# Folding the first-layer biases into the weights, one wide GELU a tile, and longer lags in a sorted two-expert kernel

## What is computed

```python
n  = layernorm(x)                               # over 128 features
a  = eps * n + adj @ n                          # per graph, 256 x 256
h  = a @ gW1 + gb1                              # 128 -> 512
h  = silu(h * rsqrt(mean(h^2) + 1e-6) * rms_w)
x  = x + h @ gW2 + gb2                          # 512 -> 128

xn = layernorm(layernorm(x)) * gamma + beta
logits = xn @ Wr + br                           # 8 experts
top 2 of the logits, softmax over the two -> w
for each expert e:                              # 128 -> 256 -> 128
    y += w[e] * (gelu(xn @ W1[e] + b1[e]) @ W2[e] + b2[e])
x  = x + y
```

## Time and profile before

| | us |
|---|---|
| median of 3 runs | 474.85 (474.79 to 475.16) |
| the profiled execution's own time | 477.58 |
| its span (first to last instruction) | 475.8 |
| PE, DVE, ACT, POOL busy | 420.9, 333.8, 294.6, 242.4 |
| mean granted TensorE clock | 0.948 |

### The profile page before, as it was taken

How to read it: one execution, slowest core, us unless ns; L and a number is a source line. 1 busy time by engine, 2 the same in 40 slices (tenths; PEclk the granted TensorE clock), 3 DMA queues, 4 the chain that set the end, 5 groups by cost and what they waited for, 6 DMA issues and landing times.

```text
span 475.8 us, 12331 instructions
## 1 busy us (share of the span) xinstructions
PE 420.9 (88%) x2944; PEld 362.1 (76%) x2944; DVE 333.8 (70%) x1398; ACT 294.6 (62%) x814; POOL 242.4 (51%) x315
## 2 busy tenths in 40 slices
PE   0969999999999999999957775999999999999980
PEld 0537777777777777877747674999989989999980
DVE  5646688887777888767847365678878878677760
ACT  1235677766666776667647342788878877555540
POOL 1112246666566766665755436356555555444550
PEclk9979999999999999999997858799999999999995
DMA  6791393323322330111145304355555543333000
GB/s 200 208 300 53 125 315 106 101 95 109 100 81 91 102 106 32 36 46 48 46 137 146 91 26 121 100 148 141 143 141 145 146 122 104 104 104 92 34 39 6
DMA packets 40892, 52.21 MB, mean 110 GB/s; under 512 B 5940, under 2 KB 35764, under 8 KB 40312
## 3 DMA queue, kind: packets, MB, share of 16 engines
q1 hardware_dynamic: 31040, 28.87, 22.3%
q0 software_dynamic: 6096, 18.52, 10.7%
q10 hardware_dynamic: 3688, 4.05, 2.8%
HBM read 36.71 MB, written 22.31 MB: 124 GB/s over the span
## 4 chain that ended last, share of the span: by engine, by line
PE 77%; DVE 8%; issue 5%; another core or an unknown queue 2%; DVEq 1%; POOL 1%; ACTq 1%; DMA 1%; ACT 1%; POOLq 0%
PE banks L678 16%; PE banks L691 16%; PE banks L556 11%; PE banks L579 10%; PE banks L543 6%; PE banks L566 5%; PE banks L597 3%; PE banks L557 3%; PE banks L589 3%; PE banks L660 2%; DVE xg L941 2%; DMA eps_col<-eps 1%; ACTq L771 1%; POOL out L501 1%
## 5 line engine op out<-in xcount | busy, mean ns | idle before, releaser
L824 ACT ACTIVATE hidden_e<-banks,b_cols 128x128 f32<-128x128 f32 x368 | 106.6, 368 | 66.8 <-PE banks L678 43.7
L501 POOL DMA_INDIRECT out<-result,rows_in x92 | 89.1, 969 | 91.0 <-DVE result L1358 84.4
L691 PE MATMUL banks<-w_sb,hidden_e 128*128 (+1 forms) x736 | 102.0, 284 | 0.2 <-issue 0.2
L691 PEld LDWEIGHTS banks<-w_sb,hidden_e 128*128 128x128 f32 x736 | 93.9, 200 | 0.8 <-issue 0.6
L464 POOL DMA_INDIRECT rows_dram<-rows_out,row_of x64 | 65.0, 1015 | 23.9 <-issue 17.3
L579 PE MATMUL banks<-gw_sb,hidden_t 128*128 128x128 f32 x512 | 69.5, 279 | 0.0
L556 PE MATMUL banks<-gw_sb,agg 128*128 128x512 f32 x128 | 68.5, 618 | 0.7 <-ACT agg L765 0.7
L579 PEld LDWEIGHTS banks<-gw_sb,hidden_t 128*128 128x128 f32 x512 | 64.3, 194 | 0.9
L742 ACT ACTIVATE hidden<-banks 128x512 f32<-128x512 f32 x64 | 38.2, 597 | 42.6 <-PE banks L557 39.4
L1344 DVE SCALAR_TENSOR_TENSOR acc<-banks,rows_in,acc 128x128 f32<-128x128 f32 x92 | 32.1, 348 | 43.5 <-PE banks L691 25.9
L907 DVE TENSOR_TENSOR hidden<-banks,rms_bc 128x512 f32<-128x512 f32 x64 | 43.8, 686 | 19.8 <-ACT hidden L742 19.8
(11 more groups left out here) (129 smaller groups left out, 737.2 us busy)
## 6 DMA issues: line engine op xcount, KB each, us to landing
rows_in<-rows_dram SPq DMA_DIRECT2D x92, 132.5 KB
adj<-adj_t SPq DMA_DIRECT2D x16, 512.0 KB, 3.7
x_tok<-x SPq DMA_DIRECT2D x16, 256.0 KB, 2.9
rows_dram<-idle_in POOLq DMA_DIRECT2D x1, 3710.0 KB, 14.2
rows_dram<-idle_in SPq DMA_DIRECT2D x28, 132.5 KB
out<-result,rows_in POOLq DMA_INDIRECT x92
w_sb<-w ACTq DMA_DIRECT2D x1, 1024.0 KB, 5.6
rows_dram<-rows_out,row_of POOLq DMA_INDIRECT x64
```

Source lines behind the costliest of these rows:

```text
L501: nc.gpsimd.indirect_dma_start(out=out, out_offset=bass.IndirectOffsetOnAxis(ap=rows_in[:, i % RING][:, IDX_AT:IDX_AT + 1].bitcast(U32), a ...
L691: last = pe.matmul(y_ps(i)[:, w], hidden_e[:, i % 4, w * HCE + c], w2_sb[:, bass.ds(at + c * D, D)], start=(c == 0), stop=(c == HCE - 1))
L824: last = nc.scalar.activation(hidden_e[:, i % 4, w * HCE + c], h_ps(2 * i + w)[:, c], ACT.Gelu, bias=b1_cols[:, bass.ds(at + c, 1)])
```

## The change

Every normalised row of 128 sums to zero. A constant added to all its elements therefore drops out against weights whose columns sum to zero, and columns that sum to something else turn that constant into a bias. The change uses this to put gb1 into gW1, and gamma, beta and b1 into W1; gamma goes into Wr, and beta @ Wr into br. The constant 1 is added where ACT copies `agg` and the turned tile (`Identity` with a bias column of ones).

```diff
-                pe.matmul(hid_ps[:, n % 3], agg[...], gw1_sb[:], start=True, stop=False)
-                pe.matmul(hid_ps[:, n % 3], bias_sel[:], bias1_parts[:], start=False, stop=True
+                pe.matmul(hid_ps[:, n % 3], agg[...], gw1_sb[:], start=True, stop=True
                           ).then_inc(hid_done, 1)
```

The sums are made on PE. The first runs before everything else in PE's queue and waits for the loads of gW1, gb1 and rms_w; the four for the experts run in steps 7 to 10, behind `aggregate`:

```diff
+            def sum_weights():
+                pe.wait_ge(wide_in, WIDE)
+                pe.wait_ge(parts_made, 1)
+                pe.matmul(hid_ps[:, 2], minus_part[:], gw1_sb[:], start=True, stop=False)
+                pe.matmul(hid_ps[:, 2], row_part[:], gb1_row[:], start=False, stop=True).then_inc(sums_done, 1)
+            def sum_beta():          # step 4, one product of 8 columns
+            def sum_expert_weights(q):
+                if q == 0:
+                    pe.wait_ge(weights_in, WEIGHTS)
+                pe.wait_ge(xg_ready, q + FOLD_AT - 4)
+                pe.matmul(feat_ps, fold_by[:], w1_sb[:, q * GT:(q + 1) * GT], start=True, stop=True
+                          ).then_inc(fold_summed, 1)
```

SP issues the expert loads, ahead of x of group 6; b1 is now broadcast to all partitions (1 MB). ACT takes over both `expert_input` (as a plain copy between its last `square` and its last `keep_turned`) and the move of the turned tile:

```diff
+                    act.wait_ge(xt_turned, i + 1)
+                    nc.scalar.activation(xg_t[:, i % 4], xt_ps(i), ACT.Identity, bias=ones[:, 0:1]
+                                         ).then_inc(xg_t_ready, 1)
-                    for w in range(2):
-                        at = expert(words, i, HCE, w == 0)
-                        act.wait_ge(h_done, 2 * i + w + 1)
-                        for c in range(HCE):
-                            last = nc.scalar.activation(hidden_e[:, i % 4, w * HCE + c], h_ps(2 * i + w)[:, c],
-                                                        ACT.Gelu, bias=b1_cols[:, bass.ds(at + c, 1)])
-                        last.then_inc(gelu_done, 1)
+                    act.wait_ge(h_done, i + 1)
+                    nc.scalar.activation(hidden_e[:, i % 4], h_ps(i), ACT.Gelu).then_inc(gelu_done, 1)
```

```diff
+WIDE_LAG, NARROW_LAG, SUM_LAG = 2, 4, 4
+AHEAD = 8
-                if (i := tile_at(step, 1)) is not None:
+                if (i := tile_at(step, WIDE_LAG)) is not None:
-                if (i := tile_at(step, 2)) is not None:
+                if (i := tile_at(step, NARROW_LAG)) is not None:
```

In `tail`, the work of group 15 from `route` on moves one step later (the table's words from step 13 to 14); on POOL `shares(NG - 1)` stands behind three results instead of six, and the scatters of group 14 ahead of the first result:

```diff
-            send_result(0)
-            send_result(1)
-            send_rows(NG - 2, (0, 1))
-            send_result(2)
-            send_rows(NG - 2, (2, 3))
-            send_result(3)
...
+            send_rows(NG - 2, (0, 1, 2, 3))
+            for i in range(3):
+                send_result(i)
             shares(NG - 1)
```

More of the change, by code:

```diff
@@ L102, in expert, with build @@
     return taken.with_bounds(min_val=0, max_val=(E - 1) * width)
-def build(nc, x, adj_t, eps, gw1, gb1, rms_w, gw2, gb2_wide, gamma, beta, wr, br, w1, b1_by_chunk, w2, b2,
+def build(nc, x, adj_t, eps, gw1, gb1, rms_w, gw2, gb2_wide, gamma, beta, wr, br, w1, b1, w2, b2,
           fixed_in, upto_in, idle_in, out):
@@ L698, in _ @@
             pe.wait_ge(table_ready, 2)
-            for step in range(TILES + 2):
+            for step in range(TILES + NARROW_LAG):
                 if step == 4:
@@ L797, in _ @@
                     square(g2, 3)
+                if g4 is not None:
+                    expert_input(g4)
                 if g3 is not None:
@@ L829, in _ @@
+                if (i := tile_at(step, WIDE_LAG)) is not None:
+                    if i >= 4:
+                        act.wait_ge(y_done, i - 3)
+                    act.wait_ge(h_done, i + 1)
+                    nc.scalar.activation(hidden_e[:, i % 4], h_ps(i), ACT.Gelu).then_inc(gelu_done, 1)
             act.wait_ge(table_ready, 2)
-            for step in range(TILES + 1):
+            for step in range(TILES + WIDE_LAG):
                 if step == EARLY:
@@ L836, in _ @@
                     normalise2(NG - 1, (2, 3))
+                if step == 4:
+                    expert_input(NG - 1)
         @block.vector
@@ L1169, in _ @@
                     weigh(g2, 1)
+                if s == 3:
+                    prep_router(1)
+                if s == 4:
+                    prep_router(2)
+                if s - FOLD_AT in range(FOLDS):
+                    fold_experts(s - FOLD_AT, 0)
                 if turned:
@@ L1337, in tile_step @@
+                    if i >= AHEAD:
+                        dve.wait_ge(result_ready, i - AHEAD + 1)
+                    nc.vector.scalar_tensor_tensor(acc[:, i % AHEAD], b2_bc[:, bass.ds(expert(words, i, D, True), D)],
                                                    rows[:, bass.ds(expert(words, i, 1, True) + W_AT, 1)],
                                                    rows[:, X2_AT:X2_AT + D], ALU.mult, ALU.add).then_inc(based, 1)
-                    tail(step, 1)
-                if (j := tile_at(step, 2)) is not None:
+                tail(step, 0)
@@ L1341, in tile_step @@
+                if (j := tile_at(step, SUM_LAG)) is not None:
+                    if j < NT and j % PER_WORD == 0:
+                        done_words[j // PER_WORD % 2] = dve.value_load(word[0:1, j // PER_WORD:j // PER_WORD + 1],
+                                                                       min_val=0, max_val=2 ** 24 - 1)
                     done = rows_in[:, j % RING]
                     dve.wait_ge(base_done, j + 1)
-                    dve.wait_ge(y_done, 2 * j + 2)
-                    nc.vector.scalar_tensor_tensor(acc[:, j % 4], y_ps(j)[:, 0],
-                                                   done[:, bass.ds(expert(words, j, 1, True) + W_AT, 1)],
-                                                   acc[:, j % 4], ALU.mult, ALU.add).then_inc(low_added, 1)
@@ L1347, in tile_step @@
[L1347 removed]
+                    dve.wait_ge(y_done, j + 1)
+                    nc.vector.scalar_tensor_tensor(acc[:, j % AHEAD], y_ps(j)[:, 0],
+                                                   done[:, bass.ds(expert(done_words, j, 1, True) + W_AT, 1)],
+                                                   acc[:, j % AHEAD], ALU.mult, ALU.add).then_inc(low_added, 1)
+                tail(step, 1)
                 if i is not None:
                     dve.wait_ge(based, i + 1)
[L1350 removed]
+                    nc.vector.scalar_tensor_tensor(acc[:, i % AHEAD], b2_bc[:, bass.ds(expert(words, i, D, False), D)],
@@ L1358, in tile_step @@
                     nc.vector.scalar_tensor_tensor(result[:, j % SENDS], y_ps(j)[:, 1],
-                                                   done[:, bass.ds(expert(words, j, 1, False) + W_AT, 1)],
-                                                   acc[:, j % 4], ALU.mult, ALU.add).then_inc(result_ready, 1)
+                                                   done[:, bass.ds(expert(done_words, j, 1, False) + W_AT, 1)],
+                                                   acc[:, j % AHEAD], ALU.mult, ALU.add).then_inc(result_ready, 1)
+                tail(step, 3)
                 tail(step, 4)
+            done_words = {}
             dve.wait_ge(table_ready, 2)
-            for step in range(TILES + 2):
+            for step in range(TILES + SUM_LAG):
                 if step == EARLY:
```

281 lines of the change are left out of this document (163 added, 118 removed).

## The result

The changed kernel takes **462.77 us** (median of 4 runs, 462.02 to 463.52) against 474.84 beside it: ratio **0.974** (95% interval 0.973 to 0.976), 12.1 us less. The forecast was 441, range 429 to 455. It was measured once more later: 464.51 against 474.75, ratio 0.979 (0.974 to 0.984). The profiled execution took 462.02 us, its span is 460.2 (before 475.8).

What follows compares the result with a forecast made beforehand. PE was taken as the bound in the group stage and near its floor in late tiles, with no engine full in the first tiles. Terms summed to -34.1 us from 477.6, less 2.7 for the median: 441 us, range 429 to 455.

Steps and rivals of the forecast that it cites:

- Bias product gone and xg moved: Group stage: dropping PE's bias products saves all 14.3 us; moving xg from VectorE to ACT saves 1.0.
- Which engine moves: Moves out of PSUM: ACT faster than VectorE for f32, 590 against 810 ns at 512 wide, against the skill page's rule.
- Folding: Steps 7 to 10: four PE products and a small beta product cost 3.5 us, eight VectorE operations 1.0.
- Start: Before the groups: earlier first Silu -4.2 us, no half-speed PE clock -2.3, two new front products with the clock -0.5.
- First tiles: First 17 tile steps: half of a possible 18 us gain taken, -9.0, bounds +4 and -18.
- the unnamed waits: First tiles: waits of 4.32 and 3.77 us for code or data, which may return and speak against the gain.
- Late tiles: Later 74 tile steps: pace falls to PE's floor, less 1.7 us for word reads; -7.3 us, between -9 and +8.
- The floor: Late tiles: PE's eight products and a transpose back to back, 1.89 us per tile.
- The end: After the last tile: last product, two additions and a scatter unchanged, 0 us.
- Profile against median: Whole kernel: the median of the runs taken as 2.7 us below the profiled time, 443.5 to 440.8.
- First tiles keep their pace: Rival, first 17 tile steps: DVE, POOL and scatters set their order, not ACT, so no gain there; 450 us, chance 0.20.
- the pace of the transposes from the 18th on: Sign in the late tiles: transposes 1.9 us apart from the 18th on.

Runs made afterwards that it cites:

- the trace with late bursts: Kernel with one register, rms apart, short lags, with results of the last 28 tiles scattered six at a time; on a chip with waits 479.78 us, ratio 1.011.

## Why the prediction was wrong

By its own steps, with what each measured.

*Bias product gone and xg moved (-14.3 and -1.0).* The mechanism was right, the size too large: 13.0 a step against 13.8, 0.8 each where 0.96 was forecast, and in three of the kernel before's steps, which took 13.4, only 0.4. From the ninth tile's widening to the first transpose the two terms gave 9.3 us; their share of the forecast was 13.5. This 4.2 us is the largest part of what is missing before the tiles. The sum took the 3.0% of the chain that the bias products had as time that would all be won.

*Which engine moves.* Right. The 512-wide move takes 595 ns on ScalarE and the 128-wide with a bias column 364, against 810 and 402 on VectorE. The Trainium skill, page "ScalarE: Activation LUTs", section "Rules for kernel authors", puts additions and multiplications on VectorE; the figure that it gives as the reason is for bf16 operations with a single source, and for these f32 moves out of PSUM the trace has ScalarE faster after the change as before it.

*Folding (+3.5 and +1.0).* 2.9 us, 1.6 less than forecast. Which part is PE's product and which VectorE's chain isn't separated: the run without folding left out both.

*Start (-4.2, -2.3, -0.5).* The half-speed stretch and the wait for Silu went. The two front products put the first aggregation 3.2 us later, where the sum had -0.5 for them and the clock together. They started late, behind a broadcast of rms that they don't need. But PE did get its full pace sooner, and by the ninth tile's widening 7.0 us were won of 8.8 forecast (the three terms, and 1.8 for eight bias products): 1.8 short. With the 4.2 above and the 1.6 that folding cost less, these are the 4.4 us missing before the tiles.

*First tiles (-9.0): this step failed.* It read idle shares and estimated a pace, and the unnamed waits stood in it as one doubt among several. They are the stage: three waits of 4 to 6 us with half-clock spells behind them, which no part of the change touches. Without them, on the other sort of chip, the 17 steps take some 43 us. 3 of the 6 us that the traces show there are only moved, since the longer lags leave three half tiles for the end.

*Late tiles (-7.3): this step failed,* and it is the largest miss, 7.8 us. The sentence that failed is "DVE loses the 0.40 move and waits on nothing new but y". The new lag brought a second load of the word into a second register, and with it register work for two of four additions, which no busy column holds: 5.5 to 7.4 us, all in tiles 20 to 63. In tiles 64 to 91, which have no such work, the pace fell from 1.99 to 1.90 as forecast. The floor itself was right, 1.896 a tile, and is reached wherever VectorE's queue has room and no waits stand in the way. The wide GELU's price was right too, 598 ns for 590. What kept the kernel before above the floor stays open. Four GELUs without the bias column (0.79 us a tile) keep it with long lags, and the wide one keeps it with short lags, both on a chip without waits. Four GELUs at their old price of 1.16 together with short lags are only in the kernel before, of which there is no trace from such a chip.

*The end (0).* Wrong by 3.3 us. A pipeline that is one step and two steps deeper has three half tiles more to empty, 2.7 us, and I had not counted them.

*Profile against median.* 3.5 us. I carried the 2.7 by which the profiled execution of before exceeded its median over to the new kernel, where the profiled execution was 0.7 below.

*The rivals.* "First tiles keep their pace" (450) came nearest, 13 us off, and with the reason I gave for it, the unnamed waits. None had VectorE's queue in the tile stage. Of the signs that the prediction named only the pace of the transposes from the 18th on failed, 2.02 us instead of 1.9.

What stays open: why a burst of scatters brings such a wait, and why on some chips only. The Trainium skill, page "Runtime: NRT & Kernel Launch", section "Instruction fetch mechanics", says that each engine fetches its code through a DMA queue of its own. A fetch stuck behind scatters would stop an engine from issuing. Against it the rows above have PE issuing for a microsecond into the wait, and in the trace with late bursts the two queues that carry instructions (q8, q14) start no packet between 418.9 and 433.4 nor between 433.4 and 452.7 us, and VectorE's waits from 426.2 to 430.2 and from 442.6 to 447.2 lie in between. So these two did not end with a fetch; for the others that isn't settled. How the changed kernel itself, unedited, does on a chip without waits wasn't measured either.

## What to carry to other kernels

Where addresses come out of registers, read an engine's queue entries in the chain of waits beside its busy time, and look at the compiled program for register instructions that an edit adds: VectorE was 68% busy in the late tiles (27.32 of 40 us from 340 to 380) and yet the bound, and in the kernel before its busy time fell when it got more work in its queue. A longer lag costs its depth once at the end, and on the chip without waits it was worth nothing. A share of the chain is the most that leaving a product out can give, not what it will give. An unnamed wait of several microseconds in the profile is a term of its own, to be forecast as "stays" until an experiment moves it, and a ratio measured on one chip should be looked at on a second.

## What the runs showed of the hardware that was not expected

- Six scatters of a 128-row tile 1.26 us apart, in tiles that otherwise run at PE's pace: on one sort of chip no effect (PE 10.00 of 10 us busy), on the other some 4 us in which VectorE and ScalarE see no product done, and PE 6.42 of 10 us busy. The kernel before takes 454.3 to 454.6 us on the one and 474 to 477 on the other.
- 416 register instructions more in VectorE's queue (1024 instead of 608: a word load for every four tiles, and the offsets of two additions) cost 9.1 us, though VectorE was busy 31.9 of 40 us at most in the stretch shown.
- Starting PE 1.2 to 1.6 us earlier at the start can bring its full clock earlier (16.9 us) or later (22.6 us), and with it the first tile 1.3 us earlier or 1.1 us later; it came later in five of seven traces.
